# A two-layer decoder on one core: GpSimd blanks a small tile behind each indirect transfer and waits for it

## The reference, cut to what matters

```
# layer 0: 8 experts of width 1024, the best 2 of sigmoid scores per token, plus a shared expert
combined = einsum('teh,te->th', eo * 0.1, w);  out = shared + combined
out = out / (max |out| + 1e-6);                x = layernorm(x + out)
# layer 1: 16 experts of width 128 in 4 groups (best 2 groups), the best 4 per token, plus 2 shared ones
routed = einsum('tef,ehf,te->th', silu(x w1) * (x w3), w2, combine)
x = layernorm(x + routed + shared)
```

## Time and profile before

| | |
|---|---|
| median of 3 timed runs | 1591.36 us (1589.53 to 1592.66) |
| profiled run | 1597.09 us |
| its span | 1595.0 us |
| mean granted TensorE clock | 0.876 |
| busy: PE, PEld, DVE, ACT, POOL | 1256.0, 813.8, 703.0, 529.6, 413.4 us |
| indirect transfers | 192, 0.96 us each: L1283 x32, L1296 x32, L2224 x64, L2240 x64 |

### The profile page before, as it was taken

One profiled execution on the slowest core, in us unless ns is written; L12 is line 12 of the kernel. 1 busy time (PEld: TensorE's weight loads), 2 busy tenths in 40 slices (PEclk: granted clock), 3 DMA queues, 4 the chain that ended last, 5 costly groups with the idle time before them and its releaser, 6 DMA issues. The chain is left out here.

```text
span 1595.0 us, 22340 instructions
## 1 busy us (share of the span) xinstructions
PE 1256.0 (79%) x6663; PEld 813.8 (51%) x6704; DVE 703.0 (44%) x1921; ACT 529.6 (33%) x999; POOL 413.4 (26%) x777
## 2 busy tenths in 40 slices
PE   6589898998788696999999998649878428983940
PEld 3244444443444574666666666535555217762730
DVE  3666575773654220222222224448746304332744
ACT  1157676777565121222222222123422002220210
POOL 4433332313333142000000005322312760034035
PEclk9679999999899597999999999679968759996985
DMA  3890000000000541111101102132000322453433
GB/s 119 293 372 14 1 0 1 0 1 1 1 1 1 202 182 43 43 32 34 35 33 34 33 20 69 44 127 100 1 0 21 129 88 87 147 160 112 145 128 96
DMA packets 74500, 117.60 MB, mean 74 GB/s; under 512 B 8160, under 2 KB 63456, under 8 KB 71456
## 3 DMA queue, kind: packets, MB, share of 16 engines
q1 hardware_dynamic: 59424, 85.94, 15.6%
q0 software_dynamic: 9216, 25.18, 4.9%
q10 hardware_dynamic: 5760, 5.25, 0.9%
HBM read 66.01 MB, written 50.33 MB: 73 GB/s over the span
## 5 line engine op out<-in xcount | busy, mean ns | idle before, releaser
L467 ACT ACTIVATE att_PT<-att_ST 128x1024 f32<-128x1024 f32 (+1 forms) x192 | 148.1, 808 | 70.4 <-PE att_ST L580 38.9
L1331 ACT ACTIVATE f_work<-f_bank,f_ub 128x128 f32<-128x128 f32 x320 | 87.1, 383 | 249.2 <-PE f_bank L1595 243.0
L499 DVE CUSTOM_DVE_ANT_0 att_junk<-att_RB,att_causal_q 128x128 f32<-128x128 f32 (+3 forms) x256 | 120.8, 487 | 64.3 <-PE att_RB L562 51.5
L1604 PE MATMUL f_bank<-wd_down,f_work 128*128 x640 | 144.8, 379 | 0.9 <-ACT f_work L1331 0.9
L1584 PE MATMUL f_bank<-wu_up,f_work 128*128 x320 | 144.1, 593 | 0.7 <-DVE f_work L1420 0.7
L562 PE MATMUL att_RB<-att_kT,att_qT 96*128 96x512 bf16 (+3 forms) x384 | 122.0, 357 | 25.1 <-DVE att_mx L499 9.2
L1604 PEld LDWEIGHTS f_bank<-wd_down,f_work 128*128 128x128 f32 x640 | 118.5, 190 | 15.6 <-issue 1.2
L1296 POOL DMA_INDIRECT wu_up<-Yd,f_pos x32 | 31.0, 968 | 365.7 <-DMA Yd<-f_work 356.5
L2549 PE MATMUL f_bank<-w_w,f_xT 128*128 x384 | 98.6, 401 | 14.7 <-DVE f_xT L2407 11.2
L1426 DVE COPY f_work<-f_bank 128x512 f32<-128x512 f32 x80 | 55.4, 692 | 123.0 <-PE f_bank L1584 123.0
L2240 POOL DMA_INDIRECT f_ga<-Yd,f_pos x64 | 61.2, 957 | 145.6 <-DMA Yd<-f_yo 110.8
(11 more groups left out here) (417 smaller groups left out, 2222.7 us busy)
## 6 DMA issues: line engine op xcount, KB each, us to landing
Xd<-g_zero SPq DMA_DIRECT2D x1, 12288.0 KB, 53.9
f_xin<-Xd SPq DMA_DIRECT2D x48, 256.0 KB
Yd<-f_yo SPq DMA_DIRECT2D x48, 256.0 KB
wu_up<-up_w SPq DMA_DIRECT2D x9, 1024.0 KB, 16.9
wd_down<-down_w SPq DMA_DIRECT2D x9, 1024.0 KB, 16.3
Xd<-g_zero SPq DMA_DIRECT2D x1, 5120.0 KB, 17.5
f_work<-Xd SPq DMA_DIRECT2D x40, 128.0 KB, 2.0
Yd<-f_work ACTq DMA_DIRECT2D x40, 128.0 KB, 1.7
```

What stands on the lines that cost most here:

```text
L467: act.activation(buf[:, :, 0:w], ST[:, 2 * (k % 2):2 * (k % 2) + 2, 0:w], ACT.Exp, scale=float(HD) ** -0.5).then_inc(exp_done, 1)
L499: dve.tensor_tensor_reduce(junk[:, k % RING, 0:w], RB[:, bank, 0:w], G.causal_q[:, 512 - w:512], 1.0, LOWEST, ALU.add, ALU.max, to).then_i ...
L1331: last = act.activation(hT[:, m, :], bank[:, TB_ + m // 4, (m % 4) * P:(m % 4 + 1) * P], ACT.Gelu, bias=ub[:, ds(e, 1), m])
L1604: mm = pe.matmul(bank[:, YB + u % 2, 0:D], hT[:, m, :], W.down[:, ds(e, 1), m, :].rearrange("p o c -> p (o c)"), start=(m == 0), stop=(m = ...
```

## The change

A tile `rest` of 128 x 16 float32 is added to both mixtures. Behind each of the 192 indirect transfers GpSimd sets it to zero and waits until that is done. Nothing reads the tile.

```diff
+    rest = sb("rest", [P, 16])                      # in moe0_stage and in moe1_stage
...
             for t in range(NT):
                 for r in range(K):
                     pool.indirect_dma_start(Xd[:, :], bass.IndirectOffsetOnAxis(pos[:, r, t:t + 1], 0),
                                             G.x_sb[:, t, :], None).then_inc(scattered, 16)
+                    ch.link(pool.memset(rest[:, :], 0.0))
...
                 for r in range(K):
                     pool.indirect_dma_start(ga[:, t, r, :], None, Yd[:, :],
                                             bass.IndirectOffsetOnAxis(pos[:, r, t:t + 1], 0)).then_inc(gathered[t], 16)
+                    ch.link(pool.memset(rest[:, :], 0.0))
...
                     for r in range(K):
                         pool.indirect_dma_start(Xd[:, :], bass.IndirectOffsetOnAxis(pos[:, n, r, s:s + 1], 0),
                                                 G.x_sb[:, TH * n + s, :], None).then_inc(scattered[n], 16)
+                        ch.link(pool.memset(rest[:, :], 0.0))
...
                     for r in range(K):
                         pool.indirect_dma_start(ga[:, s, r, :], None, Yd[0:P * R * (n + 1), :],
                                                 bass.IndirectOffsetOnAxis(pos[:, n, r, s:s + 1], 0)).then_inc(gathered[s], 16)
+                        ch.link(pool.memset(rest[:, :], 0.0))
```

More of the change, by code:

```diff
@@ L2147, in moe1_stage @@
     half = sb("half", [P, J])
+    rest = sb("rest", [P, 16])
     bank = ps("bank", [P, 8, 512])
```

## The result

The changed kernel takes 1544.65 us (median of 4 runs, 1540.68 to 1549.0); the kernel before takes 1590.44 (4 runs, 1587.31 to 1592.66). The ratio is 0.9714, 95% interval 0.9679 to 0.9749: 46 us faster. The forecast was 95 us less, 1496 us. So the sign and the kind of effect are right, and the size is half.

A forecast was written before the change was run, and what follows sets the result against it. TensorE's late reports beside GpSimd's indirect transfers were taken to bound the kernel. Gains of 17 + 19 + 44 + 35 less 8 gave 107, less 12 left in place 95: 1591.4 - 95 = 1496 us, range 1465 to 1610.

The forecast's parts named there:

- What bounds the kernel: In four stretches of GpSimd's indirect transfers, TensorE's reports come late, from some 10 us into a row; other engines' don't.
- The price of one rest: Behind each transfer, a waited memset widens the spacing by 0.25 us, to 1.52; between nothing and 0.5.
- What a pause gives back: Beside transfer rows, GpSimd offers about 0.13 us per transfer more than is carried off; a rest brings more.
- the lower end of the range: Whole kernel at 1469 us, if a rest costs nothing and has the same effect; own range from 1465.
- The sum: Gains over both mixtures' dispatches and gathers with TensorE free: 107 us, taken as 95.
- 12 left in place: Of the 115 us gained in dispatches and gathers, 12 withheld because a matmul after a pause still took 0.64 us.
- Half relief: Rival: TensorE's reports pass only at GpSimd's instruction boundaries, so 40 to 60% comes back; 1541 us, chance 20%.
- Slower: Rival: transfers as such crowd TensorE out, so rests only draw all rows out, by 48 us; 1639 us, chance 21%.
- It doesn't do what it says: Rival: the memset fits the idle 0.30 us between transfers, spacing stays 1.27; 1591 us, no effect given 7%.
- What would show it: Signs in dispatches and gathers: transfers every 1.5 us, prompt additions, 3.61 us loop steps, last gather 8 us longer.

The follow-up runs named there:

- e2: Two waited 128x16 memsets behind each indirect transfer, added to the kernel before; 1497.62 us, ratio 0.939.
- e9: The changed kernel with its memset widened from 16 to 96 columns and no rest in the last gather; 1500.45 us, ratio 0.9446 to the kernel before.
- e1: The changed kernel, but GpSimd waits only for the memset before the one just issued; 1596.25 us, ratio 0.9996 to the kernel before.
- e6: Three memsets behind each transfer in place of the change's one, each waiting only for the memset before; 1542.96 us, ratio 0.9669 to the kernel before.
- e7: Kernel before, with the first mixture's dispatch transfers carrying half of each row (128 of 256 columns); 1593.45 us, ratio 0.9994.
- e10: Kernel before, with the first mixture's dispatch transfers carrying only 64 whole rows each; 1591.72 us, ratio 1.0012.
- e4: Three waited memsets behind each transfer, where the changed kernel has one; 1525.47 us, ratio 0.9566 to the kernel before.
- e3: The changed kernel with a long waited power instruction in place of each memset; 1559.32 us, ratio 0.9776 to the kernel before.
- e11: Changed kernel with two rests in both dispatches and the loop's gather, one in the first gather, none in the last; 1481.32 us, ratio 0.9317.

## Why the prediction was wrong

**What bounds the kernel: right in the main.** TensorE's reports are late beside rows of indirect transfers. e2 takes the lateness away, and the table by windows of e9 shows the clock coming back with it. Two readings were too narrow. The other engines' reports are late too, by 1 to 2 us (e1, and VectorE in the kernel before). And the lateness doesn't start some 10 us into every row: TensorE's first gap is 8 us into the gather beside the loop (1427.21, row from 1419.14), but 17 us into the first gather and 24 us into the first dispatch.

**The price of one rest: the step that failed.** I worked out 0.25 us and a spacing of 1.52. The measured values are 0.10 and 1.37, and 0.10 is less than the 0.13 that I had estimated a rest must bring. Two rows of the sum were taken where they don't hold: 1.19 from a transfer to a computing instruction, from a single place at which the transfer itself took 1.12 (the memset follows after 0.97), and 0.19 from there to the next transfer (it is 0.28). 0.97 + 0.13 + 0.28 = 1.38 would have been right. That this step explains the miss is shown by e2, which has the spacing of the prediction and its time. The Trainium skill (Perfetto Trace Analysis, GPSIMD Engine Instruction) warns against going by durations. The trace agrees: by them alone rest and transfer fit in 1.10, and it has 1.37. My spacings came from too few rows.

**What a pause gives back: a size, at the edge.** The estimate was that 0.13 us per transfer carries the backlog off. The measured edge lies there: with +0.10 it isn't carried off in the row of 64 (`loop` 118.5) nor in the gather beside the loop (`gath2` 116.2); with +0.17 it is in the first dispatch (`disp1` 49.6) and mostly in those two (111.1 and 95.2). With +0.15 in e6's form it isn't yet (`disp1` 60.0). An estimate from a few rows could not promise so near a hit; there is luck in it. Why the loop's gather, a row of 32 too, needs more than the first mixture's stays open; it is also the row in which the lateness starts soonest. Had I set the price of a rest against this number as two quantities with an error each, 0.10 would have been an open case. Instead the lower end of the range stood for a rest that costs nothing and has the same effect, 1469, and that can't be: what a rest costs in spacing is what relieves. Nothing paid gives nothing back, as e1 shows at a spacing of 1.27.

**The sum: right, for the spacing it was made for.** e2 is the kernel that the sum describes:

| | forecast | e2 against the kernel before |
|---|---|---|
| first dispatch | 17 | 16.8 |
| first gather | 19 | 18.0 |
| second dispatch | 44 | 39.4 |
| gather in the loop | 35 | 33.1 |
| last gather | -8 | -11.4 |
| together | 107, less 12 left in place: 95 | 95.9 |

The time was 1497.6 for 1496. The 12 left in place stood for matmuls that are still slow. Of that little is found: in e2's gather beside the loop TensorE has six gaps with nothing to wait for, of 0.16 to 1.48 us, 4.0 in all. The rest are small misses in the terms; that the misses come to 11 in all, near the 12 allowed for something else, is luck. The last gather's price is higher since some of its spacings are 1.7 to 1.8 us (mean 1.67).

**Half relief.** Its 1541 us came near the result for another reason. Boundaries do nothing (e1), and the changed kernel doesn't halve the lateness all over: it nearly cures the first mixture's rows, and in the second the lateness is put off and comes back. The argument against the rival pointed the right way: each row begins in time, with the same boundaries.

**Slower.** Its first half is true in the first dispatch: it is the transfers as such, and by their number per time, not their bytes or rows (e7, e10). Its second half, that a rest only draws the rows out, holds from 1.54 us on, where e4 and e3 lose 28 and 62 us against e2. The Trainium skill (DMA: Bandwidth & Descriptors, Issuing engines are not separate DMA queues) says that the transfers of all issuing engines interleave on the same 16 DMA engines. That GpSimd's pace is therefore indifferent was my own reading, and it is wrong: the same traffic at 1.27 and at 1.54 us gives 1596.5 and 1497.6 (e2).

**It doesn't do what it says.** That describes e1, not the change: the spacing is 1.27 for the memset that isn't waited for and 1.37 for the one that is. The Trainium skill (GPSIMD Engine Reference, Instruction dispatch) says that a core of GpSimd can start the next instruction while others are still at work on the last. The trace of e6 agrees, with a memset that starts 0.05 us behind the start of one of 0.12. For a transfer behind a memset e1 shows no such overlap: it starts 0.17 us after the memset's end (598.79 and 598.96), and the memset is free only because it fits the idle time.

**What would show it.** The memset of 0.1 to 0.2 us and a longer last gather (+4.0 for 8) were seen. The spacing of 1.5, the loop's load right behind the last transfer in the first mixture (it follows the last matmul, at 623.97), the additions right behind their matmuls, the second loop's start some 53 us behind the first transfer (63.4) and 3.61 us per step through the gather were not; e2 has the load behind the transfers and the start at 54.0. I had named the late readers as the sign that I am wrong.

## What to carry to other kernels

Where GpSimd issues indirect transfers back to back beside TensorE, look for matmuls with operands and no releaser, and for readers whose wait grows along the row. If they are there, space the transfers until the growth stops and no further, and only where TensorE has something to do. Here that was 1.54 us instead of 1.27 in three of the rows and 1.37 in the first mixture's gather (e11). And when a remedy works through the time it costs, price and effect are one number. A cheap rest is a small dose, so forecast the effect as a function of the price, with the edge at which it turns.

## What the runs showed of the hardware

- Beside indirect transfers at 1.27 us spacing TensorE's reports and then its issue fall behind, at a DMA share of 0.29 and equally at 0.15 (e7), and at 53 rows per us as at 101 (e10). With waited memsets it disappears in the first dispatch between a spacing of 1.37 and 1.44 us; with e6's, which aren't all waited for, it is still there at 1.42. What inside the chip the transfers hold up isn't shown by any run.
- The reports of GpSimd and VectorE come late as well, by 1 to 2 us in the second dispatch (2.02 in e1, 1.19 and 1.24 in the kernel before).
- Late in a row TensorE's single matmuls start at distances that are multiples of about 0.7 us. In e7 they are 2.09, 2.10 and 2.80:

```profile
599.59 0.59 PE L1562 MATMUL f_bank<-wd_down,f_work 128*128 128x256 f32 x1 [1.51 <-issue]
601.68 0.58 PE L1562 MATMUL f_bank<-wd_down,f_work 128*128 128x256 f32 x1 [1.51 <-issue]
603.78 0.59 PE L1562 MATMUL f_bank<-wd_down,f_work 128*128 128x256 f32 x1 [1.52 <-issue]
606.58 0.58 PE L1562 MATMUL f_bank<-wd_down,f_work 128*128 128x256 f32 x1 [2.21 <-issue]
```

- An indirect transfer of 64 rows keeps GpSimd for 0.90 us and one of 128 for 0.97; rows of half the length change nothing (0.97 in e7). Cutting a transfer in two would nearly double the issue time, by an estimate from the spacings: 2 x 1.20 us for 1.27.
- A waited memset behind a transfer costs 0.10 us at 16 columns and 0.17 at 96, and a second one of 16 columns costs 0.17 more. A single one that isn't waited for costs nothing (e1), three such cost 0.15 (e6).
